# A decoder layer's second stage: x1 added in PSUM by an identity matmul, with four PSUM banks in turn

## The reference, cut to what matters

```python
x = layernorm(x + attn(x))            # stage 1 -> x1
x = layernorm(x + xattn(ctx, x))      # stage 2 -> x2
x = layernorm(x + ffn(x))             # stage 3 -> output
```

## Time and profile before

| | us |
|---|---|
| median of 3 runs | 3185.77 (3181.36 to 3189.07) |
| the profiled execution | 3179.85 |
| its span | 3178.1 |
| PE busy | 2833.5 (89%) |
| DVE busy | 2746.7 (86%) |
| ACT busy | 737.8 (23%) |
| POOL busy | 602.2 (19%) |

### The profile page before, as it was taken

One profiled execution on the slowest core, in us unless ns is written; L12 is line 12 of the kernel. 1 busy time (PEld: TensorE's weight loads), 2 busy tenths in 40 slices (PEclk: granted clock), 3 DMA queues, 4 the chain that ended last, 5 costly groups with the idle time before them and its releaser, 6 DMA issues. The chain is left out here.

```text
span 3178.1 us, 81270 instructions
## 1 busy us (share of the span) xinstructions
PE 2833.5 (89%) x30692; PEld 2261.9 (71%) x30692; DVE 2746.7 (86%) x8246; ACT 737.8 (23%) x1302; POOL 602.2 (19%) x604
## 2 busy tenths in 40 slices
PE   7960067699999999999999999999999999999997
PEld 5850045477778787878787878787877787878776
DVE  5667877799989999989999999999898999999974
ACT  4720034222212222222221222222222222222210
POOL 1320000122212122212222222212222222222221
PEclk9975556899999999999999999999999999999998
DMA  5550036000000000000000000000000000000000
GB/s 171 175 145 0 0 109 204 19 2 12 12 12 12 12 12 12 12 12 12 12 12 12 12 12 12 12 12 12 12 12 12 12 12 12 12 12 12 8 8 8
DMA packets 88596, 94.14 MB, mean 30 GB/s; under 512 B 6109, under 2 KB 86910, under 8 KB 88062
## 3 DMA queue, kind: packets, MB, share of 16 engines
q1 hardware_dynamic: 88206, 88.74, 9.1%
HBM read 60.94 MB, written 27.79 MB: 28 GB/s over the span
## 5 line engine op out<-in xcount | busy, mean ns | idle before, releaser
L970 POOL TENSOR_TENSOR hot_lo<-hot_lo,valsT 128x512 f32<-128x512 f32 x512 | 538.6, 1052 | 2398.0 <-DVE hot_lo L1227 2398.0
L1020 PE MATMUL bank<-x2T,dnT 128*64 128x256 f32 x8192 | 985.3, 382 | 0.4 <-ACT gelh L1122 0.4
L1043 PE MATMUL bank<-up,gelh 128*128 128x256 f32 x4096 | 896.1, 380 | 2.8 <-DVE gelh L1238 2.8
L1043 PEld LDWEIGHTS bank<-up,gelh 128*128 128x128 f32 x4096 | 779.3, 190 | 135.2 <-issue 28.7
L1225 DVE TENSOR_TENSOR hot_hi<-iota,valsT 128x1024 f32<-128x1024 f32 x512 | 825.8, 1613 | 15.9 <-ACT valsT L1117 15.9
L1020 PEld LDWEIGHTS bank<-x2T,dnT 128*64 128x64 f32 x8192 | 601.6, 138 | 192.7 <-issue 12.8
L1033 PEld LDWEIGHTS bank<-hot_lo,hot_hi 128*64 128x64 f32 x16384 | 587.3, 140 | 127.8 <-issue 74.7
L1033 PE MATMUL bank<-hot_lo,hot_hi 128*64 128x64 f32 x16384 | 584.0, 224 | 62.2 <-DVE gelh L1238 26.4
L1122 ACT ACTIVATE gelh<-bank 128x512 f32<-128x512 f32 x512 | 305.8, 598 | 813.3 <-PE bank L1020 812.6
L1238 DVE TENSOR_TENSOR gelh<-bank,gelh 128x512 f32<-128x512 f32 x512 | 348.6, 681 | 80.8 <-PE bank L1033 53.0
L1227 DVE TENSOR_TENSOR hot_lo<-offs,valsT 128x512 f32<-128x512 f32 x512 | 352.3, 688 | 0.0
(11 more groups left out here) (145 smaller groups left out, 1958.1 us busy)
## 6 DMA issues: line engine op xcount, KB each, us to landing
x_scratch<-x_sb SPq DMA_DIRECT2D x64, 256.0 KB, 2.2
xT_sb<-in_xT SPq DMA_DIRECT2D x32, 256.0 KB, 2.8
x_sb<-in_x SPq DMA_DIRECT2D x32, 256.0 KB, 2.8
x_again<-x_scratch SPq DMA_DIRECT2D x32, 256.0 KB, 2.7
x_tile<-x_scratch SPq DMA_DIRECT2D x32, 256.0 KB, 3.0
x_res<-x_scratch SPq DMA_DIRECT2D x32, 256.0 KB, 3.2
out_y<-yo SPq DMA_DIRECT2D x32, 256.0 KB, 2.4
gelh<-in_table SPq DMA_DIRECT2D x4, 1024.0 KB, 8.9
```

Of the source, the lines that this page charges most:

```text
L970: pool.tensor_tensor(hot_lo[:, slot(q)], hot_lo[:, slot(q)], valsT[:, par, 2, TQ * q:TQ * (q + 1), None].to_broadcast([P, TQ, 2 * CL]), AL ...
L1020: mm = pe.matmul(ps_h[q % 2][rows, c, :], dnT[:, k, 2 * q + c, rows], x2T[:, k, :, :].rearrange("p a t -> p (a t)"), start=(k == 0), stop= ...
L1043: mm = pe.matmul(ps_out[:, a, :], gelh[:, par, c, a, :], up[:, c, :], start=(c == 0), stop=(c == CL - 1))
```

## The change: what it does

- PE's `warp` adds, for each row tile, a second matmul into the same accumulation: the 128 by 128 identity as weights and the x1 tile as the moving operand (`start=False, stop=True`). PSUM then holds ctx part plus x1. `warp` therefore also waits for the load of x1.
- DVE's `add` and the buffer `y2` go. `stats` waits for `warp_mm` and reads PSUM; ACT's `norm` reads PSUM.
- The sum stays in its bank until `norm` has read it, so four banks are used in turn (1, 2, 5, 6), and `warp` of b waits for `norm` of b-4 in place of `add` of b-2. `pipeline` hands the step's number down, and a stage may ask for it modulo 4 (its third entry); ACT's and PE's loops are unrolled 4 times with 8 steps written out ahead (before: 2 and 6).
- SP's `load` of b waits for `warp` of b-2 in place of `add` of b-2.

```diff
-            def step(i, par):
-                for stage, lag in stages:
+            def step(i, lane):
+                for stage, lag, *lanes in stages:
...
-                        stage(b, (par + lag) % 2)
+                        stage(b, (lane - lag) % (lanes[0] if lanes else 2))
...
-            y2 = sw("y2", [P, 2, NT, C])
...
-            ps_warp = [bank[1 + i][:, :].rearrange("p (t c) -> p t c", t=NT) for i in range(2)]
+            ps_warp = [bank[i][:, :].rearrange("p (t c) -> p t c", t=NT) for i in (1, 2, 5, 6)]
...
                 def load(b, par):
                     if later(b, 2):
-                        sp.wait_ge(sum2_done, b - 1)
+                        sp.wait_ge(warp_mm, b - 1)
...
-                def norm(b, par):
+                def norm(b, lane):
+                    par = lane % 2
...
-                        last = act.activation(x2_sb[:, par, t, :], y2[:, par, t, :], ACT.Identity,
+                        last = act.activation(x2_sb[:, par, t, :], ps_warp[lane][:, t, :], ACT.Identity,
...
-                pipeline(act, [(norm, 4), (ramps, 0), (std, 3)], 6)
+                pipeline(act, [(norm, 4, 4), (ramps, 0), (std, 3)], 8, unroll=4)
...
-                def warp(b, par):
-
+                def warp(b, lane):
+
+                    par = lane % 2
                     pe.wait_ge(mask_ready, b + 1)
-                    if later(b, 2):
-                        pe.wait_ge(sum2_done, b - 1)
+                    pe.wait_ge(x1_in[par], dmas(b, par))
+                    if later(b, 4):
+                        pe.wait_ge(x2_ready, b - 3)
                     for t in range(NT):
-                        mm = pe.matmul(ps_warp[par][:, t, :], mask[:, par, t * P:(t + 1) * P],
-                                       ctx_rows[:, bass.ds(b, 1), :].rearrange("s a c -> s (a c)"),
-                                       start=True, stop=True)
+                        pe.matmul(ps_warp[lane][:, t, :], mask[:, par, t * P:(t + 1) * P],
+                                  ctx_rows[:, bass.ds(b, 1), :].rearrange("s a c -> s (a c)"),
+                                  start=True, stop=False)
+                        mm = pe.matmul(ps_warp[lane][:, t, :], ident[:, :], x1_sb[:, par, t, :], start=False, stop=True)
                     mm.then_inc(warp_mm, 1)
...
-                pipeline(pe, [(turn, 4), (warp, 1)], 6)
+                pipeline(pe, [(turn, 4), (warp, 1, 4)], 8, unroll=4)
...
-                def add(b, par):
+                def stats(b, lane):
                     dve.wait_ge(warp_mm, b + 1)
-                    dve.wait_ge(x1_in[par], dmas(b, par))
-                    if later(b, 2):
-                        dve.wait_ge(x2_ready, b - 1)
-                    dve.tensor_tensor(y2[:, par], ps_warp[par], x1_sb[:, par], ALU.add).then_inc(sum2_done, 1)
-
-                def stats(b, par):
                     for t in range(NT):
-                        dve.bn_stats(out=st2[:, par, t, :], in_=y2[:, par, t, :])
+                        dve.bn_stats(out=st2[:, lane % 2, t, :], in_=ps_warp[lane][:, t, :])
...
-                pipeline(dve, [(add, 2), (recip, 3), (settle, None), (masks, 0), (shift, 3), (chan_stats, 5),
-                               (stats, 2), (settle, None), (aggr, 2)], 8, unroll=4)
+                pipeline(dve, [(recip, 3), (settle, None), (masks, 0), (shift, 3), (chan_stats, 5),
+                               (stats, 2, 4), (settle, None), (aggr, 2)], 8, unroll=4)
```

More of the change, by code:

```diff
@@ L129, in decoder_layer @@
         warp_mm = sem("warp_mm")
-        sum2_done = sem("sum2_done")
         shift2_ready = sem("shift2_ready")
@@ L200, in step @@
                     if not isinstance(b, int) or 0 <= b < total:
-                        stage(b, (par + lag) % 2)
+                        stage(b, (lane - lag) % (lanes[0] if lanes else 2))
             for i in range(peel):
-                step(i, i % 2)
+                step(i, i)
             with eng.Fori(0, (total - peel) // unroll) as j:
                 for u in range(unroll):
-                    step(j * unroll + (peel + u), (peel + u) % 2)
-            for i in range(total, total + max(lag or 0 for _, lag in stages)):
-                step(i, i % 2)
+                    step(j * unroll + (peel + u), peel + u)
+            for i in range(total, total + max(lag or 0 for _, lag, *_ in stages)):
+                step(i, i)
         def dmas(b, par):
```

## The result

| | before | after |
|---|---|---|
| median of 4 runs | 3186.39 us | 3148.84 us |
| profiled execution | 3179.85 us | 3147.87 us |
| its span | 3178.1 us | 3146.2 us |
| second block: first ramp to the channels' aggregation | 109.9 us | 104.2 us |
| third block: two groups, between `y3` of the same loop parity, mean of 13 | 160.8 us | 158.8 us |

The two last rows (read from starts in the two traces: first `ramps`, the aggregation at 528.43 and 522.82, and the 32 starts of the third block's residual add) say where it lies: the second block gives 5.7 us, as forecast, and the third block, which I had let "just shift", gives 26.3 of the span's 31.9.

The account below looks back on a forecast made before the run. DVE's own instruction sequence was taken to set the second block's step. Start +1.3, loop -6.9 and behind it -0.85 gave -6.45 us: 3173.4 us against the profiled execution, 3179.3 against the median, range 3173 to 3192.

Parts of the forecast that it names:

- The add and the trip to ACT: DVE's second-block loop: without add, aggr to recip takes 0.61 us in plain steps; -1.23 us per turn of the loop.
- The jump step: DVE's step where its second-block loop jumps back: aggr to recip taken as 0.64 us, 0.61 if the jump costs nothing beyond.
- Statistics from PSUM: DVE's stats in the second block reading PSUM in place of SBUF: +0.02 us per step, +0.08 per turn.
- The start: Start of the second block's pipeline: first shift +1.7 us from slower first products, +1.3 left by the fifth shift.
- Behind the loop: Second block after DVE's loop: two recip that still came behind an add gain -0.85 us for both.
- The clock: PE in the second block: clock rises in the first two or three sequences and stays, so DVE remains the bound.
- rival (1): Second block: clock stays at 1.2 GHz and PE becomes the bound; +35 us, 3221 us, chance 0.12.
- Sum of the second block: All terms for the second block together: +1.3 - 6.9 - 0.85 = -6.45 us.
- the first step: Opening claim: the change can move about 100 us of 3178, the second block's pipeline; the climb and third block just shift.

Follow-up runs that it names:

- e4: Changed kernel with 95 semaphore increments on PE, so PE's third-block loop begins exactly at a piece's beginning: 3138.4 us, ratio 0.9844.
- e11: Changed kernel with 95 PE increments again, same as e4, run beside e10 on one chip: 3139.4 us, ratio 0.9864.
- e2: Changed kernel with 80 PE increments, putting PE's third-block loop at the unpadded kernel before's place in a piece: 3181.7 us, ratio 0.9980.
- e7: e4 with the third block's loop over four groups a turn in place of two, half as many jumps: 3138.8 us, ratio 0.9852.
- e6: Changed kernel without the identity matmuls, x1 left out of the sum, waits kept: 3144.9 us (one execution).
- e8: Kernel before with only PE's and ACT's second-block loops unrolled 4 times, 8 steps ahead, add kept on DVE: 3146.2 us, ratio 0.9876.
- e1: Kernel before with 176 PE increments, putting PE's third-block loop at the unpadded changed kernel's place in a piece: 3156.5 us, ratio 0.9901.
- e10: Kernel before with 15 PE increments, so PE's third-block loop begins exactly at a piece: 3144.2 us, ratio 0.9879.
- e3: Kernel before with 256 PE increments, one whole piece, leaving the loop's place within a piece as it was: 3185.6 us, ratio 0.9992.

## Why the prediction was right and wrong

- **The add and the trip to ACT: right.** 0.61 in each plain step, with 0.36 of it waiting for ACT. The jump step came out at 0.61, the bound, not 0.64. The loop's step fell from 3.349 to 3.068, 24 x 0.281 = 6.7 us; the forecast had 6.9.
- **Statistics from PSUM: right**, 0.74 and 0.75 for a pair. The 62 cycles that the Trainium skill (VectorE: DVE Perf Modes, TRN2 errata) gives to a PSUM source don't show in them.
- **The start: right in its sum, by luck.** The fifth `shift` came at 438.22, 1.3 us later counted from the first ramp, as forecast. The way there was another: the first `shift` was only 0.9 later (the clock rose at 424.5, in the second product), the rest came between the fourth and the fifth. DVE's timeline of the kernel after:

```profile
426.31 0.15 DVE L815 SCALAR_TENSOR_TENSOR nb<-mv,rs 128x2 f32<-128x2 f32 x1
...
434.94 0.48 DVE L796 SCALAR_TENSOR_TENSOR mask<-iota,bounds,ramp 77x256 f32<-77x256 f32 x1 [1.16 <-PE bank L695]
...
438.22 0.15 DVE L815 SCALAR_TENSOR_TENSOR nb<-mv,rs 128x2 f32<-128x2 f32 x1
```

  The mask waited 1.16 us for a product before which PE had stood idle 1.77 us, until 432.86. That was one late load: the fifth sequence's x1, issued at 428.44, landed at 432.77, after 4.33 us, where the loads take 2.7. In e4 and e11 it took 2.70 and 2.84, PE started 0.1 us behind its landing there too, and the fifth `shift` came 1.0 and 1.2 us earlier, at 18.6 and 18.4 us from the first ramp, about as the kernel before (18.3). So the +1.3 is this execution's; e2 and e7 had +0.5 and +1.0.
- **Behind the loop:** -0.3 (what is left of -5.7 after +1.3 and -6.7) in place of -0.85. At the end the clock had fallen again (at 520.1); whether that is the reason was not tried.
- **The clock: right in its course**, and rival (1) fell with it. It mattered less than I said: without the added matmuls the step is the same at 1.2 GHz (e6), so the faster clock is only the condition under which they are free.
- **Sum of the second block:** -5.7, and with the same second block -4.4 (e2, where the clock fell once), -7.2 (e4), -6.0 (e7) and -6.8 (e11), against -6.45.
- **What failed is the first step, in one clause:** "what is ahead of it (the climb) and behind it (the third block ...) just shifts with its end". The third block's instructions and their order did not change, but their place in PE's program did, and its time from the aggregation to the end fell by 26.3 us of the span's 31.9. None of the terms of the sum (+1.3, -6.9, -0.85) was for the place of a loop in the program; it stood at nothing without a reason. Where the edit put unrolled steps ahead of it I had written that they cost nothing, "the unrolled loops of PE and ACT jump half as often, in their idle time: nothing": that was true of the second block and false of the kernel. e8 has that edit alone, at -37 us with the second block at its 109.9; e1 has the bare shift of 176 instructions, at -34 in the medians.
- The pause was in the trace of before, 35.7 us in all on PE under the names POOL and issue, each time at the jump (2.3 to 3.3 us). I read the chain and the stretches only where the code was edited.

## What to carry to other kernels

A long loop whose program comes in anew at every turn (here 16 or 17 pieces of 16 KB on PE's queue) can pay for each jump back, and how much depends on where the loop begins within a piece: here 2.7 us per jump with 15 instructions to the next boundary, 0.9 with 95, under 0.1 from 191 on. Between 95 and 191 nothing was tried. Any edit ahead of such a loop shifts it, so before crediting an edit with a gain (or a loss) in a part that it does not touch, pad both kernels to the same place: this change is worth 4.8 us by itself; the other 33 of its 37.6 come from the loop's new place, and 15 idle instructions in the kernel before give 38. When an instruction is taken from between two halves of a round trip, price the bare trip, and look for another instruction to put over it (masks first: 7 us more).

## What was not expected of the hardware

- The cost of a loop's place: 38 us of 3186 (1.2%) for 15 instructions (e10), back again after a whole piece of 256 (e3).
- Once the boundary is far enough, DVE's own jump remains: its first instruction behind the branch comes 2.75 to 3.2 us after it at every taken jump of all kernels (0.1 us in the last pass, which is not taken), and a jump costs the group 0.7 us (e4 against e7).
- PE is on its way back early: its branch starts while old matmuls still run and lasts 3.3 to 3.9 us when it is taken, 0.08 when it is not.
- The clock stayed at 1.2 GHz over 440 to 500 with PE busy 58.3 of 60 us (e6), and from 438.7 to 451.5 it was busy 12.80 of 12.8 us, transposes among the matmuls. It rose 4.8 us after the first product began when two products ran on without a gap (after), but not in the 5.54 us of the kernel before. What decides it stays open here.
